# A graph build on TensorE: ranges read into registers once a tile, two blocks a table word, and a running counter

## The chip, the cores and the metric

One core of one Trainium2 chip. The metric is the device time of one execution in microseconds (us). The core's engines are TensorE (PE, with its weight loads PEld), VectorE (DVE), ScalarE (ACT), GpSimd (POOL) and SyncE (SP). Each has a sequencer that takes its instructions in order. Some of them never reach the engine behind it: register arithmetic, a load of registers from memory, branches, waits. In the trace these have the engine's name with a q (PEldq, DVEq).

## What is computed

Four graph layers over 1250 nodes of 512 features and 20,000 edges, each with a residual and a layer norm. Cut to what matters here:

```python
edge_index = stack([src, dst])                      # dst is sorted
x = layernorm(x + L0(x, edge_index, edge_weight))   # segment_sum(support[src] * weight, dst)
x = layernorm(x + L1(x, edge_index, edge_type_2))   # two relational layers: segment_sum over edges of each type
x = layernorm(x + L2(x, edge_index))                # normalised by degree
x = layernorm(x + L3(x, edge_index, edge_attr_8))   # attention over edges, 8 heads
```

The kernel does not gather rows of nodes. It first builds dense matrices of 1280 x 1280 (edge weights for L0 as a high and a low f16 part, edge counts of each of the two types for L1), and the layers are then matmuls with them. The change is in this build alone.

## The kernel before, in words

The 20,000 edges are 160 chunks (CH) of 125 edges, in the order of their destination. The destinations are 40 blocks of 32 nodes (TT = 40, CW = 32), four blocks to a tile (t4, 10 tiles). A block's rows of all matrices are a product: for each chunk that holds edges of the block, `own` (125 edges x 128: which of the 32 nodes, times four values) is PE's stationary operand, and a one-hot row over the 1250 other nodes is the moving one. DVE makes that row by comparing an iota with a key (line 878 for fixed visits, line 886 for further ones). One chunk is one visit: three matmuls of 512, 512 and 226 columns at line 1617, into three banks of PS.

A block has four fixed visits (FIXED = 4), and further ones in a loop whose length depends on the data. There are 44 further ones over 40 blocks: 36 blocks have one, four have two. The range of a block's chunks is worked out on the chip: a column of 40 words (first chunk, number of further visits, and an offset with which the running number of a further visit is the chunk plus the offset) is written to DRAM and read back into one row, `tab`. `tile_ranges` (line 436) loads four words into registers at each tile start, on DVE and on PE apart (line 439 is where the load and its checks stand in the trace). A range's shifts and masks are written where they are used.

The order of the work in one block on PE (`build`, line 1611): wait `evicted` (line 1626), first fixed visit, loop over the further visits (line 1628: wait `more_made`), then `fix` of the block before (line 1605: wait `copied`, three matmuls at line 1607 that take the copied high part off), then three fixed visits, and the signal `built`. ACT evicts each block twice: line 1320 copies 128 rows (signal `copied`; it waits for `built`), and line 1322, behind the fix, copies what is left in 32 rows (signal `evicted`). Blocks take turns on two sets of three banks, so block j waits for the eviction at line 1322 of block j-2; and the fix inside block j waits for the copy at line 1320 of block j-1. DVE (`make`, line 873) waits `built` of block j-2 for its eight fixed rows (HOTS), and `more_used` for its two further ones (MORE = 2). Semaphores are compared with registers (`wait_ge(more_made, v + 1)`). POOL's zero fills of a DRAM table (line 730) start on `built`; SP writes the evicted blocks out (lines 579 and 581) and starts the next weights' loads after the last.

The loops are loops of the chip, not unrolled: over the tiles (line 1644 on PE, lines 897 and 906 on DVE) and over the further visits (`Fori(lo + FIXED, hi)`). The build runs from 68.0 us, when PE's first matmul of it starts, to 243.6 us.

Of the kernel before, what the change touches and what calls it, by code (L numbers as in the profile page):

```python
# [8 lines left out]
I32 = mybir.dt.int32  # L9
ALU = mybir.AluOpType  # L10
# [10 lines left out]
EC = 125  # L21
CH = EDGES // EC
# [38 lines left out]
def gnn_resnorm(nc, a, out):  # L61
    ctx = ExitStack()
    with ctx:
# [11 lines left out]
        tab_d = dram("tab_d", (1, TT), I32)  # L75
# [45 lines left out]
        tab = in_w(TT)[0:1, :].bitcast(I32)  # L121
# [314 lines left out]
        def tile_ranges(eng, t4):  # L436

            ap = tab[:, bass.ds(t4 * 4, 4)]
            _, vals = nc.values_load_multi_w_load_instructions(ap, engines=(eng.engine,), min_val=0,
                                                                max_val=2 ** 31 - 1)  # L440
# [93 lines left out]
        def _(sp):  # L534
# [28 lines left out]
            sp.dma_start(tab_d[0, :].rearrange("(t k) -> t k", k=1), tabi[0:TT, 0:1]).then_inc(tab_out, 16)  # L563
            sp.wait_ge(tab_out, 17)
            sp.dma_start(tab, tab_d).then_inc(tab_in, 16)
# [207 lines left out]
        def _(dve):  # L773
# [9 lines left out]
            dve.sem_inc(more_made, CH)  # L783
# [60 lines left out]
            dve.wait_ge(ext_t, 2)  # L844
            step(V.tensor_tensor(bound[0:TT, 0:1], PS[0:TT, 3, 0:1], lohi[0:TT, 1:2], ALU.subtract))
            step(V.tensor_scalar(bound[0:TT, 0:1], bound[0:TT, 0:1], float(CH), None, ALU.add))
            V.tensor_copy(tabi[0:TT, 0:1], bound[0:TT, 0:1])
            V.tensor_copy(tabi[0:TT, 1:2], lohi[0:TT, 0:1])
            step(V.tensor_copy(tabi[0:TT, 2:3], visits[0:TT, :]))
            for k in range(2):  # L850
                step(V.tensor_scalar(tabi[0:TT, 0:1], tabi[0:TT, 0:1], 8, None, ALU.logical_shift_left))
                step(V.tensor_tensor(tabi[0:TT, 0:1], tabi[0:TT, 0:1], tabi[0:TT, k + 1:k + 2], ALU.bitwise_or))
# [19 lines left out]

            def make(rng, t4, j):

                lo, hi, off = rng
# [7 lines left out]
                with dve.Fori(lo + FIXED, hi) as c:  # L883
                    v = c + off
# [4 lines left out]
                for m in range(1, FIXED):  # L889
                    fixed(m)  # L890
# [1218 lines left out]
```

## Time and profile before

| | us |
|---|---|
| median of 3 runs | 1287.15 (1283.82 to 1288.16) |
| the profiled execution, its own time | 1289.35 |
| its span | 1287.6 |
| the build in it | 175.6, from 68.0 to 243.6 |
| PE busy, of the span | 1214.6 (94%) |
| DVE / ACT / POOL busy | 862.7 / 419.6 / 306.5 |
| granted TensorE clock, mean | 0.987 |

Some 1.8 us of the profiled execution lie around its span. A duration of a register instruction is its execution alone; the time from one to the next is longer, and the "issue" entries in the trace are idle time of an engine for which the trace shows no other releaser. A matmul's duration holds its passage through the array; the next one can start before it ends.

### The profile page before, as it was taken

The page shows a single profiled execution, that of the slowest core. Times are in us where ns is not written, and L with a number is a line of the kernel's source. Part 1 is how long each engine was busy: PE and PEld are TensorE (multiplying, and loading weights), DVE is VectorE, ACT ScalarE, POOL GpSimd, SP SyncE. Part 2 cuts the span into 40 slices and gives each one's busy share as a digit, 9 for nine tenths or more (in the row PEclk, how much of TensorE's full clock was granted, in tenths as well). Part 3 has the DMA queues.
Part 4 walks back from the last instruction along what each step waited for, and adds up shares of the span by engine and source line. Part 5 has one row for each costly group of instructions (what it writes and reads, how often), then busy time and mean ns, then how long its engine had stood idle before and what let it go on. Part 6 is the DMA issues. An engine that isn't in the chain of part 4 may idle for free.

```text
span 1287.6 us, 22149 instructions
## 1 busy us (share of the span) xinstructions
PE 1214.6 (94%) x8447; PEld 549.6 (43%) x8448; DVE 862.7 (67%) x1178; ACT 419.6 (33%) x564; POOL 306.5 (24%) x220
## 2 busy tenths in 40 slices
PE   6988888999898999999999999999999999999997
PEld 2333333333343334444444454453333555555553
DVE  7576665534434565562478873758999787978787
ACT  2445555522133122212301002154442343433432
POOL 2011010000010234354555555555461000000000
PEclk9989999999998999999999999999999999999999
DMA  8568886598698888734122212122323655556452
GB/s 307 217 220 264 283 290 186 191 395 314 217 371 294 292 287 271 257 76 131 14 38 34 50 20 49 2 24 32 43 32 100 221 206 197 169 182 207 154 181 103
DMA packets 64411, 222.77 MB, mean 173 GB/s; under 512 B 31224, under 2 KB 36088, under 8 KB 48358
## 3 DMA queue, kind: packets, MB, share of 16 engines
q1 hardware_dynamic: 34792, 156.40, 35.5%
q0 software_dynamic: 25184, 53.10, 16.5%
q10 hardware_dynamic: 4350, 12.07, 2.7%
q8 instruction: 63, 1.03, 0.3%
q14 instruction: 22, 0.18, 0.0%
HBM read 198.94 MB, written 59.94 MB: 201 GB/s over the span
## 4 chain that ended last, share of the span: by engine, by line
PE 72%; DVE 10%; issue 8%; DMA 7%; ACT 2%; DVEq 1%; SPq 1%; ACTq 1%
PE PS L1738 23%; PE PS L1687 10%; PE PS L1617 8%; PE PS L1983 5%; PE PS L1970 5%; PE PS L1553 4%; DVE R L1123 4%; PE PS L2016 3%; PE PS L1571 3%; PE PS L2003 2%; PE PS L1852 2%; PE PS L1607 2%; DMA W<-w_d 2%; DVE R L1158 1%; DMA w_d<-W 1%
## 5 line engine op out<-in xcount | busy, mean ns | idle before, releaser
L764 POOL DMA_INDIRECT bias_d<-R x160 | 268.8, 1680 | 333.1 <-DMA bias_d<-R 221.4
L1738 PE MATMUL PS<-R 128*128 128x512 f16 x1300 | 298.1, 381 | 0.0
L1738 PEld LDWEIGHTS PS<-R 128*128 128x128 f16 x1300 | 120.4, 98 | 180.7 <-issue 49.7
L1617 PE MATMUL PS<-R,XX 125*128 125x512 f16 (+2 forms) x612 | 130.9, 347 | 24.9 <-DVE R L878 16.1
L1518 ACT ACTIVATE R<-PS 128x1024 f32<-128x1024 f32 (+1 forms) x100 | 100.5, 1005 | 163.7 <-PE PS L1970 163.6
L1158 DVE SCALAR_TENSOR_TENSOR R<-R,W 128x1024 f32<-128x1024 f32 (+1 forms) x68 | 134.6, 1990 | 14.4 <-ACT R L1518 13.0
L1687 PE MATMUL PS<-W,XX 128*128 128x512 f16 x600 | 134.4, 383 | 4.8 <-DVE R L961 2.7
L878 DVE TENSOR_SCALAR R<-W,R 125x1250 f16<-125x1250 f16 x160 | 89.5, 606 | 46.9 <-PE PS L1617 43.3
L1123 DVE CUSTOM_DVE_ANT_0 R<-PS,R 128x1250 f16<-128x1250 f32 x80 | 116.8, 1459 | 5.5 <-PE PS L1906 2.9
L1983 PE MATMUL PS<-R 128*32 128x256 f32 (+1 forms) x1600 | 105.7, 382 | 5.0 <-DVE R L1158 4.2
L1970 PE MATMUL PS<-R 128*128 128x256 f16 (+3 forms) x800 | 106.0, 274 | 1.3 <-DVE R L1123 1.1
L730 POOL DMA_DIRECT2D bias_d<-bias_d x39 | 22.7, 589 | 324.7 <-PE PS L1617 153.5
L1617 PEld LDWEIGHTS PS<-R,XX 125*128 x612 | 57.5, 99 | 93.7 <-issue 57.0
L961 DVE SCALAR_TENSOR_TENSOR R<-PS,gate,R 128x512 f16<-128x512 f32 x50 | 37.4, 750 | 88.3 <-ACT R L1373 88.3
L1970 PEld LDWEIGHTS PS<-R 128*128 128x128 f16 (+1 forms) x800 | 71.6, 99 | 50.2 <-ACT R L1518 31.1
L1687 PEld LDWEIGHTS PS<-W,XX 128*128 128x128 f16 x600 | 57.8, 99 | 75.3 <-issue 7.5
L1158 DVE SCALAR_TENSOR_TENSOR R<-R 128x1024 f32<-128x1024 f32 (+1 forms) x32 | 63.6, 1993 | 9.3 <-ACT R L1518 5.5
L1322 ACT ACTIVATE R<-PS 32x1280 f32 x40 | 49.2, 1231 | 62.6 <-PE PS L1607 62.6
L1356 ACT ACTIVATE stat<-stat 128x1 f32<-128x1 f32 x30 | 8.8, 295 | 184.1 <-DVE stat L949 184.1
L1373 ACT ACTIVATE R<-PS,gate 128x512 f16<-128x512 f32 x50 | 34.4, 687 | 96.2 <-PE PS L1687 95.5
L1852 PE MATMUL PS<-XX,W 128*128 128x512 f16 (+1 forms) x288 | 61.3, 345 | 1.1 <-ACT R L1474 1.1
L1738 PE MATMUL PS<-W,XX 128*128 128x512 f16 x240 | 58.1, 387 | 3.0 <-issue 3.0
(220 smaller groups left out, 1357.0 us busy)
## 6 DMA issues: line engine op xcount, KB each, us to landing
bias_d<-bias_d POOLq DMA_DIRECT2D x39, 1280.0 KB, 10.7
R<-in_basis_s SPq DMA_DIRECT2D x32, 1024.0 KB, 6.8
W<-in_basis_s SPq DMA_DIRECT2D x28, 1024.0 KB, 6.6
W<-bias_d SPq DMA_DIRECT2D x27, 1024.0 KB, 4.9
R<-bias_d SPq DMA_DIRECT2D x13, 1024.0 KB, 4.8
R<-key_d SPq DMA_DIRECT2D x20, 500.0 KB, 3.7
R<-R SPq DMA_DIRECT2D x120, 80.0 KB, 6.3
W<-bias_d SPq DMA_DIRECT2D x7, 904.0 KB, 4.6
```

The lines of the kernel that those rows point to most:

```text
L764: pool.indirect_dma_start(bias_d, bass.IndirectOffsetOnAxis(ap=idx[:, c:c + 1], axis=0), attr[:, c, :], None, bounds_check=DUMP + GC * P - ...
L878: V.tensor_scalar(hot[0:EC, FIXED * (j % 2) + m, 0:NODES], iota16[0:EC, 0:NODES], base[0:EC, bass.ds(t4, 1), j], key[0:EC, bass.ds(lo + m, ...
L1123: V.tensor_tensor_reduce(out=junk[:, 0:NODES], in0=PS[:, b0:b0 + 3, :].rearrange("p a b -> p (a b)")[:, 0:NODES], in1=nmask[:, i, 0:NODES] ...
L1158: V.scalar_tensor_tensor(p, p, BIG, BR[t % NB].rearrange("p (r h) -> p h r", h=HEADS)[:, 4 * q:4 * q + 4, 0:w], ALU.min, ALU.mult).then_in ...
L1518: S.activation(ER[:, n % 4, :].rearrange("p (h r) -> p h r", h=4)[:, :, 0:w], PS[:, 2 * (n % 2):2 * (n % 2) + 2, :].rearrange("p a (e r) - ...
L1553: ins = T.matmul(PS[32 * c:32 * c + RELS * FT, MIXED(m), :], attbd[0:BJ, layer, :, :].rearrange("p r j -> p (r j)"), BASIS(m)[0:BJ, c, :], ...
L1617: ins = T.matmul(mm_out(3 * (j % 2) + b, p1 - p0), own[0:EC, bass.ds(c, 1), :, :].rearrange("p c m w -> p (c m w)"), hots(p0, p1), start=f ...
L1687: ins = T.matmul(mm_out(zi % 2, D), lhs, rhs, start=n == 0, stop=n == len(terms) - 1)
L1738: ins = T.matmul(mm_out(SUM_BANK(s, i), D), lhs, rhs, start=n == 0, stop=n == len(terms) - 1)
L1852: ins = T.matmul(mm_out(BANK_OF("q", g), hi - lo), W16[:, 1 + which, q, f, o_ * P:(o_ + 1) * P], XT16[:, p, f, lo:hi], start=n == 0 and f ...
L1970: ins = T.matmul(PS[:, 2 * (n % 2) + i // 2, (i % 2) * RB:(i % 2) * RB + w], key[:, h, j * P:(j + 1) * P], query[:, h, cols], start=k == 0 ...
L1983: ins = T.matmul(PS[32 * i:32 * i + 32, 4 + q, e * RB:e * RB + w], VA[:, j, 4 * q + i, 32 * e:32 * e + 32], ER[:, n % 4, i * RB:i * RB + w ...
```

## The change

1. A word of the table holds two blocks, 16 bits each (first chunk in the upper 8, further visits in the lower 8); the offset is gone, and with it the DVE steps that made it. The column is written to DRAM in 2-byte elements. DVE and PE load two words a tile, not four.
2. All four ranges of a tile are shifted, masked and kept in registers at the tile start, on both engines.
3. The loop over further visits runs from 0 to their count. Its running number is a register `visited`, which each engine adds one to at the loop's foot; `more_used` and `more_made` start from other values to match.

```diff
-        def tile_ranges(eng, t4):
-            ap = tab[:, bass.ds(t4 * 4, 4)]
+        def tile_ranges(eng, t4, regs):
+            ap = tab[:, bass.ds(t4 * 2, 2)]
...
-            for p in vals:
-                first = within((p >> 8) & 255, 0, CH - FIXED - 1)
-                end = within(first + (p & 255) + FIXED, FIXED + 1, CH)
-                ranges.append((first, end, eng.snap(p >> 16)))
+            for j in range(4):
+                part = []
+                for bit in (8, 0):
+                    reg = regs[len(part) + 2 * j]
+                    eng.reg_alu(reg, vals[j // 2], bit + 16 * (j % 2), ALU.logical_shift_right)
+                    eng.reg_alu(reg, reg, 255, ALU.bitwise_and)
+                    part.append(reg)
+                ranges.append((eng.snap(part[0], min_val=0, max_val=CH - FIXED - 1),
+                               eng.snap(part[1], min_val=1, max_val=CH)))
...
-            step(V.tensor_tensor(bound[0:TT, 0:1], PS[0:TT, 3, 0:1], lohi[0:TT, 1:2], ALU.subtract))
-            step(V.tensor_scalar(bound[0:TT, 0:1], bound[0:TT, 0:1], float(CH), None, ALU.add))
...
-                with pe.Fori(lo + FIXED, hi) as c:
-                    v = c + off
+                with pe.Fori(0, count) as n:
+                    v = pe.snap(visited, min_val=0, max_val=TT * CH)
                     pe.wait_ge(more_made, v + 1)
-                    visit(c, lambda p0, p1: flat(more[0:EC, bass.ds(v & (MORE - 1), 1), p0:p1]),
+                    visit(within(lo + FIXED + n, FIXED, CH - 1),
+                          lambda p0, p1: flat(more[0:EC, bass.ds(v & (MORE - 1), 1), p0:p1]),
                           False).then_inc(more_used, 1)
+                    pe.reg_add(visited, visited, 1)
```

(`make` on DVE changes in the same way.)

**PE at a tile's start** (tiles 1 to 9), from the table's load to the first visit's matmuls; an ISA row here is a check or several register operations packed into one instruction. Before:

```order
L439 TENSOR_LOAD W
L439 ISA x8
L1626 REGISTER_ALU
L1623 ISA [waits evicted]
L1617 REGISTER_ALU [waits hot_made]
L1617 REGISTER_ALU
L1617 ISA
L1617 MATMUL PS<-R,XX 128x512 x2
```

And now; the four rows behind the first L450 stand three times, for the ranges of the other three blocks:

```order
L440 TENSOR_LOAD W
L440 ISA x4
L447 REGISTER_ALU
L448 REGISTER_ALU
L447 REGISTER_ALU
L448 REGISTER_ALU
L450 ISA
L448 REGISTER_ALU
L447 REGISTER_ALU
L448 REGISTER_ALU
L450 ISA
...
L1633 ISA [waits evicted]
L1627 ISA [waits hot_made]
L1627 MATMUL PS<-R,XX 128x512 x2
```

Between the load and the first matmul stood 13 instructions, and now stand 23: half of the checks are gone, and 13 single register operations and four packed ones have come.

**PE at the loop over further visits** of any block. Before:

```order
L1628 ISA
L1628 UNCONDITIONAL_BRANCH
L1628 ISA
L1617 REGISTER_ALU [waits more_made]
L1617 ISA
L1617 REGISTER_ALU
L1617 MATMUL PS<-R,XX 128x512
...
L1628 REGISTER_ALU x2
L1628 ISA
L1628 COMPARE_AND_BRANCH
```

And now (a plain move of a register, which these rows don't show, stands ahead of the branch):

```order
L1638 UNCONDITIONAL_BRANCH
L1638 ISA
L1627 REGISTER_ALU [waits more_made]
L1627 ISA x2
L1627 MATMUL PS<-R,XX 128x512
...
L1644 ISA
L1638 COMPARE_AND_BRANCH
```

At the loop's foot three register instructions became one, and at its head one packed instruction became a move. A later block's start (blocks 1 to 3 of a tile) loses two of the four register instructions between its waits and its first matmul.

## Rows read from the trace of the kernel before

**Rows 1.** The page: the chain that ended last, by line.

```profile
PE PS L1738 23%; PE PS L1687 10%; PE PS L1617 8%; PE PS L1983 5%; PE PS L1970 5%; PE PS L1553 4%; DVE R L1123 4%; PE PS L2016 3%; PE PS L1571 3%; PE PS L2003 2%; PE PS L1852 2%; PE PS L1607 2%; DMA W<-w_d 2%; DVE R L1158 1%; DMA w_d<-W 1%
```

**Rows 2.** The build's stretch: busy time by engine (columns in its first row).

```profile
core 0: us, PE busy (x) PEld busy (x) DVE busy (x) ACT busy (x) POOL busy (x), PEclk, DMA share, GB/s
...
68.00:243.60 175.60, 152.25 (x730) 65.98 (x731) 116.15 (x210) 96.26 (x78) 15.35 (x24) 0.97 0.74 234
```

**Rows 3.** Line 1617, the build's matmuls: a sequencer instruction (ns), PE's idle time (us, count).

```profile
L1617 PEldq ALU_OP  x168: 32/36/47, 67.7 to 240.5; - x168
...
  issue: 65.3, 122
```

**Rows 4.** Timeline: blocks 2 and 3 of tile 4, start of tile 5 (start us, duration us).

```profile
149.72 1.23 ACT L1322 ACTIVATE R<-PS 32x1280 f32 x1 [1.19 <-PE PS L1607]
151.22 1.24 ACT L1320 ACTIVATE R<-PS 128x1280 f16<-128x1280 f32 x1 [0.26 <-PE PS L1617]
...
151.41 1.37 PE L1617 MATMUL PS<-R,XX 125*128 125x512 f16 x6 [0.23 <-issue]
...
152.83 0.70 PE L1607 MATMUL PS<-R,W 128*128 128x512 f16 x3
...
156.24 1.42 PE L1617 MATMUL PS<-R,XX 125*128 125x512 f16 x6 [1.13 <-DVE R L878]
```

**Rows 5.** Line 439 on PE's sequencer at the start of tile 5 (min/median/max ns).

```profile
L439 PEldq FUSED_REGOPS  x4: 146/152/168, 154.6 to 155.5; - x4
L439 PEldq SEQ_ASSERT  x4: 18/18/18, 154.8 to 155.7; - x4
L439 PEldq TENSOR_LOAD <-W x1: 434/434/434, 154.0 to 154.0; - x1
```

**Rows 6.** Line 1628, head and foot of the loop over visits, on PE's sequencer.

```profile
L1628 PEldq FUSED_REGOPS  x128: 41/78/157, 68.0 to 241.1; - x128
...
L1628 PEldq COMPARE_BRANCH  x44: 67/67/214, 69.3 to 241.2; - x44
```

**Rows 7.** Timeline of PE: a further visit behind the first.

```profile
109.27 0.69 PE L1617 MATMUL PS<-R,XX 125*128 x3 [0.69 <-issue]
```

**Rows 8.** Timeline of PE: tile starts (idle before in brackets), and one fix (L1607).

```profile
85.63 1.39 PE L1617 MATMUL PS<-R,XX 125*128 125x512 f16 x6 [0.83 <-issue]
...
174.73 1.42 PE L1617 MATMUL PS<-R,XX 125*128 125x512 f16 x6 [1.54 <-DVE R L878]
...
191.97 1.49 PE L1617 MATMUL PS<-R,XX 125*128 125x512 f16 x6 [1.73 <-DVE R L878]
...
198.73 0.70 PE L1607 MATMUL PS<-R,W 128*128 128x512 f16 x3 [0.36 <-ACT R L1320]
...
211.44 1.42 PE L1617 MATMUL PS<-R,XX 125*128 125x512 f16 x6 [1.22 <-DVE R L878]
...
228.06 1.39 PE L1617 MATMUL PS<-R,XX 125*128 125x512 f16 x6 [1.10 <-DVE R L878]
```

**Rows 9.** Timeline of ACT: the eviction ahead of that fix.

```profile
197.43 1.24 ACT L1320 ACTIVATE R<-PS 128x1280 f16<-128x1280 f32 x1 [1.35 <-PE PS L1617]
```

**Rows 10.** Timeline of DVE: the first two blocks of tile 2.

```profile
98.19 0.61 DVE L878 TENSOR_SCALAR R<-W,R 125x1250 f16<-125x1250 f16 x1 [1.24 <-PE PS L1617]
...
102.07 0.61 DVE L878 TENSOR_SCALAR R<-W,R 125x1250 f16<-125x1250 f16 x1 [0.95 <-PE PS L1617]
```

**Rows 11.** Line 439 on DVE's sequencer, all tiles.

```profile
L439 DVEq FUSED_REGOPS  x40: 183/186/224, 65.4 to 222.7; - x40
```

**Rows 12.** Busy time and granted clock (PEclk) behind three of PE's idle times.

```profile
175.40:179.00 3.60, 3.25 (x18) 1.51 (x18) 1.09 (x3) 1.56 (x2) 0.16 (x1) 1.00 0.77 200
193.20:196.60 3.40, 3.35 (x11) 1.33 (x10) 0.27 (x1) 1.23 (x1) 0.00 (x0) 0.50 0.71 172
328.40:335.00 6.60, 4.80 (x29) 1.27 (x29) 2.51 (x4) 2.39 (x4) 0.00 (x0) 1.00 0.26 41
```

**Rows 13.** Timeline of PE: the idle time at 328.4 us.

```profile
330.26 1.04 PE L1553 MATMUL PS<-R,attbd 120*8 120x512 f32 x8 [1.80 <-DVE W L929]
```

More of the change, by code:

```diff
@@ L9 @@
 I32 = mybir.dt.int32
+I16 = mybir.dt.int16
 ALU = mybir.AluOpType
@@ L120, in gnn_resnorm @@
         iota16 = in_w(NN // 2).bitcast(F16)
-        tab = in_w(TT)[0:1, :].bitcast(I32)
+        tab = in_w(TT // 2)[0:1, :].bitcast(I32)
         fix16 = in_w(P // 2).bitcast(F16)
@@ L843, in _ @@
             step(V.tensor_tensor(valA[0:EC, :, 2], wgt[0:EC, :], valA[0:EC, :, 3], ALU.subtract))
-            dve.wait_ge(ext_t, 2)
-            step(V.tensor_tensor(bound[0:TT, 0:1], PS[0:TT, 3, 0:1], lohi[0:TT, 1:2], ALU.subtract))
-            step(V.tensor_scalar(bound[0:TT, 0:1], bound[0:TT, 0:1], float(CH), None, ALU.add))
[L847 to L852, printed above, removed]
+            V.tensor_copy(tabi[0:TT, 0:1], lohi[0:TT, 0:1])
+            step(V.tensor_copy(tabi[0:TT, 1:2], visits[0:TT, :]))
+            step(V.tensor_scalar(tabi[0:TT, 0:1], tabi[0:TT, 0:1], 8, None, ALU.logical_shift_left))
+            step(V.tensor_tensor(tabi[0:TT, 0:1], tabi[0:TT, 0:1], tabi[0:TT, 1:2], ALU.bitwise_or))
             V.tensor_copy(inside[0:TT, 0:1], visits[0:TT, :]).then_inc(tab_out, 1)
@@ L871, in _ @@
             dve.wait_ge(tab_in, 16)
+            visited = dve.alloc_register("visited")
+            range_regs = [dve.alloc_register(f"range_{i}") for i in range(8)]
+            dve.reg_mov(visited, 0)
             def make(rng, t4, j):
-                lo, hi, off = rng
+                lo, count = rng
                 def fixed(m):
@@ L882, in make @@
                 fixed(0)
-                with dve.Fori(lo + FIXED, hi) as c:
-                    v = c + off
+                with dve.Fori(0, count) as n:
+                    v = dve.snap(visited, min_val=0, max_val=TT * CH)
                     dve.wait_ge(more_used, v + 1)
                     V.tensor_scalar(flat(more[0:EC, bass.ds(v & (MORE - 1), 1), 0:NODES]), iota16[0:EC, 0:NODES],
-                                    base[0:EC, bass.ds(t4, 1), j], key[0:EC, bass.ds(c, 1)], ALU.add,
+                                    base[0:EC, bass.ds(t4, 1), j],
+                                    key[0:EC, bass.ds(within(lo + FIXED + n, FIXED, CH - 1), 1)], ALU.add,
                                     ALU.is_equal).then_inc(more_made, 1)
+                    dve.reg_add(visited, visited, 1)
                 for m in range(1, FIXED):
@@ L892, in windows @@
             def windows(t4):
-                rngs = tile_ranges(dve, t4)
+                rngs = tile_ranges(dve, t4, range_regs)
                 for j in range(4):
@@ L1598, in _ @@
             pe.wait_ge(wl_made, M0)
-            pe.sem_inc(more_used, CH + MORE)
+            pe.sem_inc(more_used, MORE)
             pe.sem_inc(built, 2)
@@ L1609, in fix @@
                 ins.then_inc(fixed_up, 1)
+            visited = pe.alloc_register("visited")
+            range_regs = [pe.alloc_register(f"range_{i}") for i in range(8)]
+            pe.reg_mov(visited, 0)
             def build(rng, j, t4, first):
-                lo, hi, off = rng
+                lo, count = rng
                 def visit(c, hots, first):
```

12 lines of the change are left out of this document (5 added, 7 removed).

## The prediction, made before the changed kernel had run

> **What bounds the kernel now.** First the page's chain of waits by line: the build's matmuls (L1617) hold 8% and its fixes (L1607) 2% [rows 1]; the rest is layers that the change does not touch. Then the build as one stretch: 175.6 us, PE busy 152.25 of them, DVE 116.15 and ACT 96.26 [rows 2]. So PE sets the pace and 23.4 us of it are pauses (its idle time by releaser in one line: 65.3 us in 122 entries are "issue", which count what lies under a matmul's passage too, so they are no sum to save [rows 3]). Then the timeline, for where the pauses are. There are two kinds.
>
> At a tile's start PE stands 0.83 us (first of nine), 1.54, 1.73, 1.22, 1.10 (last) [rows 8]; the nine make a mean of 1.28. The trace puts most down to DVE's line 878, but DVE works two blocks ahead (it waits for `built` of block j-2): it makes the first row of tile 2 at 98.19, after 1.24 us of waiting for PE, and the next block's at 102.07, waiting again [rows 10]. The semaphore of DVE had long been there. What ends last is PE's own sequencer: the load of the ranges at 154.04 takes 0.434, eight checks and five further instructions follow, and the first matmul stands at 156.24 [rows 4, 5]: 1.77 us behind the load's end.
>
> Inside a tile a block takes about 3.9 us. The eviction of 32 rows ends at 150.95, the block's first matmul starts at 151.41: 0.46 of register work. ACT's copy ends at 152.46, the fix starts at 152.83 [rows 4]; where the fix had nothing else to wait for it came 0.06 behind the copy (198.67 to 198.73) [rows 8, 9]. So a ring of PE and ACT with about 0.3 us of register slack in it.
>
> **The price of a register instruction.** The 13 between load and matmul executed for 4 x 0.152 (checks), 4 x 0.018 (asserts) [rows 5], 3 x 0.036 [rows 3] and two small packed ones at 0.05: 0.89 us of the 1.77. The rest over 13 is 0.065 each between one and the next. So: single ALU 0.10, check 0.217, assert 0.083, packed from 0.106 (0.041 the shortest) to 0.233 (0.168 the dearest) [rows 5, 6]. The Trainium skill ("Perfetto Trace Analysis", Sequencer-only Instruction) says that the profiler shows the execution alone and that a hidden tail hangs on every sequencer operation; by execution alone the tile's start would lengthen by half as much as below, and the trace agrees with the page, half of the 1.77 being unseen.
>
> **Part by part.**
>
> 1. Table. The DVE steps for the offset lie in the preparation ahead of the build, with DVE waiting behind them, and the table lands long before 64 us: nothing, either way. If that cover were gone it would be some eight small DVE steps, under 1 us.
>
> 2. Ranges at a tile's start, PE. Now 2 checks (0.434), 2 asserts (0.166), 13 ALU (1.30), the last two packed (0.233) = 2.13, and four packed ones whose contents I can't see: 0.42 to 0.93 for the four; I take 0.73, 0.18 each, nearer the checks since they too pack a bound. 2.86 against 1.77: **+1.09 us a tile start** (bounds +0.78 to +1.29; below that only if single ALUs in a row overlapped, which the 0.065 says they do not). The load itself, two words instead of four, is one instruction before and after: no change taken. Nothing hides it, as PE waits for nothing else. Nine times: +9.8.
>
> 3. The same on DVE: its checks are dearer (0.186 each of 40 [rows 11]), four go a tile, the shifts come: about +0.9 us. DVE waits 1.24 and 0.95 us on PE in each block [rows 10], so it is hidden, but for tile 0, where PE waits for the first row: +0.3 net.
>
> 4. Counter, PE. Foot of the loop: two ALU fewer, -0.19. Head: the first packed one (0.078 median) becomes a move, the second (up to 0.157, it holds the offset's shift) gets lighter, a single one turns packed: -0.08 (0.04 to 0.12) [rows 6]. A visit's matmuls now stand 0.69 after the block's first ones [rows 7].
>
> 5. Start of blocks 1 to 3: two register instructions fewer between wait and matmul, -0.19.
>
> Could all of 4 and 5 be had, it were 0.27 in block 0 and 0.46 in blocks 1 to 3. But once the fix is 0.06 behind ACT's copy, ACT sets it: a one-visit block gives at most 0.37 - 0.06 = 0.3. I take 0.27, 0.17 (block 1, where the copy starts later), 0.30, 0.30: 1.04 a tile. So a tile is +1.09 - 1.04 = +0.05; nine: +0.5. The four blocks with two visits have more room (fix long behind the copy): 0.4 more each, -1.6. With tile 0's +0.3 the registers come to **-0.8 us**: a wash, gains inside tiles, losses at their starts.
>
> **What the longer pauses do to the clock.** This decides the sign. PE's granted clock stood at 0.50 for the stretch from 193.20, behind the pause of 1.73 before 191.97, and at 1.00 behind those of 1.54 (stretch from 175.40) and of 1.80 (before 330.26) [rows 8, 12, 13]. So near 1.7 us it can go either way. What it costs: tiles of two-visit blocks took 19.47 us (191.97 to 211.44) with the fall and 18.49 (156.24 to 174.73) without [rows 4, 8]; their closing pauses were 1.22 and 1.54, so a fall is worth 0.98 + 0.32 = 1.3 us. The new pauses are 1.28 + 1.09 = 2.37 in the mean (1.9 to 2.8): all longer than the one that fell. One of two around 1.75 fell; 2.37 lies further out than both, and tile 0's or a short pause behind it may save some. I take **4 of 9**, less the one there is: 3 x 1.3 = +3.9.
>
> Sum: -0.8 + 3.9 = +3.1. The profiled execution was 1289.35, its span 1287.6, and 2.2 above the median of 1287.15; the difference goes on the median: **1290.2 us**. Behind the build all waits for the last block's store, so a shift of its end passes on one to one; loads that have more time ahead could give some back, taken at nothing.
>
> **Rivals.**
>
> A. The clock falls at nearly every tile start (8 of 9), and packed instructions cost the upper value (nine times +0.2 = +1.8). 7 x 1.3 = 9.1, + 1.8 - 0.8 = +10.1: 1297.2. For it: every new pause is above 1.73, and a half-clock block makes its own ring longer. Against: 1.80 stayed at full clock. It is slower than before by more than can be told from about four additional falls on.
>
> B. No further falls, registers as worked out: 1286.4. The rise in pauses is 1.1 us and PE is over 80% busy around them; 1.54 and 1.80 did nothing.
> The Trainium skill ("TensorE: Matmul & The Clock Gate", What's actually happening) has the clock fall only after a window of idleness; pauses under 3 us, as here, would by it do nothing, so it speaks for B. The fall behind 1.73 us [rows 12] speaks against it.
>
> C. Faster: single ALUs in a row and the packed ones at their cheapest (nine times -0.31 = -2.8), registers -0.8, and the fall at 191.97 gone by a shift in phase (-1.3): -4.9: 1282.3. Nothing but luck in phase speaks for the last, the first needs packed ones as light as the lightest.
>
> D. DVE's longer chain reaches PE: only if it has less lead than 1.24 + 0.95 us somewhere; then nine times 0.9 = 8.1 less the registers' 0.8: +7.3, 1294.5. The waits of rows 10 speak against it.
>
> E. The change doesn't do what it says, for instance a range that makes an additional or a missing visit: the sum of visits comes from the same numbers, so it could only show as other matmul counts; I give it nothing.
>
> **How the numbers follow.** Forecast 0.38, A 0.26, B 0.20, C 0.12, D 0.04. About 3.9 us (0.3%) is what a measurement can tell from no change. Faster: C and a little of B with light packed ones, 0.18. Slower: A and D, and the part of the forecast with five or more falls, 0.37. Same: 0.45. The range runs from near C to A: 1283 to 1297; the likeliest case's own is 1287 to 1293.
>
> **What would show it.** PE's pauses at tile starts about 2.4 us (1.1 longer than before), the first matmul 2.9 us behind the load's end. In a block with one visit, the fix 0.06 to 0.1 behind ACT's copy; block period 3.6 to 3.7. The granted clock at 0.50 in about four places just behind tile starts; the build 173.5 to 183 us long, about 178.7. The DVE still waits for PE in each block. Wrong it would be if pauses stay under 2 us (the price of a register instruction), if the block's period stays at 3.9 (the ring), if the clock falls nowhere or everywhere, or if the time moves outside the build.

## The result, and the profile after

| | before | after |
|---|---|---|
| median, 20 runs each | 1287.39 | 1294.81 |
| ratio | 1 | 1.0049 (1.0036 to 1.0062), +6.3 us (the medians differ by 7.4) |
| the profiled execution's span | 1287.6 | 1293.6 |
| the build in it | 175.6, from 68.0 | 180.3, from 68.95 |
| mean granted TensorE clock, all runs | 0.9870 (17 runs) | 0.9821 (20 runs) |
| falls of the clock between tile 1 and the build's end | 1 | 6 |

The kernel became slower. The forecast was 1290.2, +3.1 and within what can't be told from no change; rival A said 1297.2. The time, 1294.8, is inside the range of 1283 to 1297, 4.6 above the forecast and 2.4 below rival A. The 17 runs of before with a clock are those of the first chip job below; all kernels of one job share them.

The page's chain by line, and the build as one stretch [rows 1, 2] (columns as there):

```profile
PE PS L1750 23%; PE PS L1699 10%; PE PS L1627 7%; PE PS L1995 5%; PE PS L1982 5%; PE PS L1559 4%; DVE R L1129 4%; PE PS L2028 3%; PE PS L1577 3%; PE PS L2015 2%; PE PS L1864 2%; PE PS L1613 2%; DMA W<-w_d 2%; DVE R L1164 1%; DMA w_d<-W 1%
```

```profile
68.95:249.24 180.29, 154.58 (x730) 68.76 (x731) 115.06 (x210) 96.22 (x78) 13.75 (x24) 0.93 0.71 228
```

The shares have hardly moved, and DVE and ACT are as busy as they were. The build is 4.7 us longer, and its granted clock fell from 0.97 to 0.93. What lies behind the build took 1044.4 us, against 1044.0: a shift passes on one to one, as said.

Line 1627 is what line 1617 was [rows 3]. PE has 44 single operations there in place of 168, yet more idle time under "issue":

```profile
L1627 PEldq ALU_OP  x44: 32/36/36, 69.4 to 245.9; - x44
...
  issue: 72.9, 115
```

Blocks 2 and 3 of tile 6 [rows 4] in the timeline (start us, duration us):

```profile
184.97 3.14 PE L1627 MATMUL PS<-R,XX 125*128 125x512 f16 x15
...
186.76 1.24 ACT L1326 ACTIVATE R<-PS 128x1280 f16<-128x1280 f32 x1 [0.25 <-PE PS L1627]
...
188.06 0.70 PE L1613 MATMUL PS<-R,W 128*128 128x512 f16 x3
```

ACT's copy ends at 188.00, the fix starts at 188.06: the 0.37 of before is now 0.06, what it was before only where nothing else held the fix. And from 184.97 to the next fix PE runs 15 matmuls over the block's border without a pause, where 0.2 stood. Inside a tile the counter and the prepared ranges did all that was forecast.

The start of tile 1, line 440 on PE's sequencer [rows 5], and then all tiles on both engines [rows 11]:

```profile
L440 PEldq TENSOR_LOAD <-W x1: 556/556/556, 83.5 to 83.5; - x1
```

```profile
L440 PEldq TENSOR_LOAD <-W x10: 538/898/1554, 64.3 to 231.5; - x10
L440 DVEq TENSOR_LOAD <-W x10: 544/547/1456, 64.4 to 227.3; - x10
```

From the load's end (83.49 + 0.556 = 84.05) to the first matmul (86.73) it is 2.68 us; 1.77 before. That was forecast as 2.86. But look at the load: two words take 0.547 us on DVE in the median, and on PE four of the nine at tile starts take 1.2 to 1.6. Before, with four words:

```profile
L439 PEldq TENSOR_LOAD <-W x10: 362/584/1032, 65.0 to 225.9; - x10
...
L439 DVEq TENSOR_LOAD <-W x10: 352/362/615, 64.8 to 221.5; - x10
```

I had put the load down as unchanged.

The loop over visits [rows 6]: each packed instruction of 0.078 or 0.157 is now 0.047, and the move is 0.029.

```profile
L1638 PEldq FUSED_REGOPS  x44: 47/47/52, 69.1 to 245.8; - x44
...
L1638 PEldq MOVE  x40: 29/29/37, 69.0 to 245.7; - x40
```

PE's nine tile starts [rows 8] (idle before in brackets):

```profile
86.73 1.43 PE L1627 MATMUL PS<-R,XX 125*128 125x512 f16 x6 [1.84 <-issue]
...
103.53 1.90 PE L1627 MATMUL PS<-R,XX 125*128 125x512 f16 x6 [2.24 <-issue]
...
123.06 1.33 PE L1627 MATMUL PS<-R,XX 125*128 125x512 f16 x6 [3.16 <-issue]
...
142.22 2.26 PE L1627 MATMUL PS<-R,XX 125*128 125x512 f16 x6 [2.98 <-DVE R L882]
...
160.07 1.36 PE L1627 MATMUL PS<-R,XX 125*128 125x512 f16 x6 [2.17 <-DVE R L882]
...
179.47 1.33 PE L1627 MATMUL PS<-R,XX 125*128 125x512 f16 x6 [2.14 <-DVE R L882]
...
196.78 2.26 PE L1627 MATMUL PS<-R,XX 125*128 125x512 f16 x6 [2.82 <-DVE R L882]
...
216.61 2.15 PE L1627 MATMUL PS<-R,XX 125*128 125x512 f16 x6 [3.09 <-DVE R L882]
...
234.75 1.33 PE L1627 MATMUL PS<-R,XX 125*128 125x512 f16 x6 [2.17 <-DVE R L882]
```

Their mean is 2.51 us, 1.28 before. Again most are put down to DVE, which is no more the cause than it was: at tile 2 its own register chain is now the 1.80 us ("issue"), and it still waits 3.17 us for PE within the tile [rows 10].

```profile
98.79 0.61 DVE L882 TENSOR_SCALAR R<-W,R 125x1250 f16<-125x1250 f16 x1 [1.80 <-issue]
...
105.86 0.61 DVE L890 TENSOR_SCALAR R<-W,R 125x1250 f16 x1 [3.17 <-PE PS L1627]
```

The clock [rows 12]: stretches behind pauses of 2.98, 2.17 and 2.14 us (tiles 4, 5 and 6), with the granted clock after the counts:

```profile
142.22:145.10 2.88, 2.88 (x8) 1.18 (x9) 0.00 (x0) 0.00 (x0) 0.00 (x0) 0.50 0.85 222
162.20:165.60 3.40, 3.40 (x12) 1.40 (x11) 1.83 (x4) 1.23 (x1) 0.00 (x0) 0.51 0.57 124
179.50:182.90 3.40, 3.40 (x18) 1.54 (x18) 0.78 (x2) 1.23 (x1) 0.00 (x0) 1.00 0.80 209
```

Six of the nine pauses were followed by a fall (tiles 2, 3, 4, 5, 7, 8), three were not (1.84, 2.14, 2.17).

### The profile page after: what moved, and what is told of

Read it like the earlier page. It is cut to its first block, busy times and chain, and to the rows that moved or that the text cites. A ratio compares the mean times of both kernels' runs of the same rounds, so it can differ in the third digit from the quotient of the medians.

```text
span 1293.6 us, 22050 instructions
## 1 busy us (share of the span) xinstructions
PE 1216.7 (94%) x8447; PEld 552.4 (43%) x8448; DVE 860.1 (66%) x1173; ACT 419.2 (32%) x564; POOL 307.6 (24%) x220
## 3 DMA queue, kind: packets, MB, share of 16 engines
q8 instruction: 63, 1.03, 0.3%
## 4 chain that ended last, share of the span: by engine, by line
PE 71%; DVE 10%; issue 8%; DMA 6%; ACT 2%; DVEq 1%; ACTq 1%; SPq 0%
PE PS L1750 23%; PE PS L1699 10%; PE PS L1627 7%; PE PS L1995 5%; PE PS L1982 5%; PE PS L1559 4%; DVE R L1129 4%; PE PS L2028 3%; PE PS L1577 3%; PE PS L2015 2%; PE PS L1864 2%; PE PS L1613 2%; DMA W<-w_d 2%; DVE R L1164 1%; DMA w_d<-W 1%
## 5 line engine op out<-in xcount | busy, mean ns | idle before, releaser
L770 POOL DMA_INDIRECT bias_d<-R x160 | 271.6, 1697 | 336.9 <-DMA bias_d<-R 224.0
```

Of the source, the lines that this page charges most:

```text
L770: pool.indirect_dma_start(bias_d, bass.IndirectOffsetOnAxis(ap=idx[:, c:c + 1], axis=0), attr[:, c, :], None, bounds_check=DUMP + GC * P - ...
```

## The experiments

Four kernels ran in each of the first two jobs and three in the last, with the kernel before run beside them. Times are medians; ratios are to the kernel before of the same job, with 95% intervals. Pauses, loads and falls are those of one profiled execution of each kernel. All have the tile loop, the blocks and the data as they were; none leaves out any of the computation.

| kernel | median, us | ratio | mean clock of its runs | PE's nine pauses at tile starts, sum in its profile, us |
|---|---|---|---|---|
| before (three jobs) | 1288.8, 1288.3, 1287.6 | 1 | 0.9870, 0.9870, 0.9873 | 11.5 |
| changed kernel | 1294.8 | 1.0049 (1.0036 to 1.0062) | 0.9821 | 22.6 |
| counter only | 1282.2 | 0.9953 (0.9938 to 0.9968) | 0.9865 | 11.3 |
| ranges only | 1296.6 | 1.0061 (1.0038 to 1.0084) | 0.9822 | 26.0 |
| ranges spread | 1279.2 | 0.9922 (0.9903 to 0.994) | 0.9863 | 11.4 |
| spread, load ahead | 1277.2 | 0.9903 (0.9884 to 0.9923) | 0.9880 | 0.4 |
| no checks | 1287.0 | 0.9991 (0.997 to 1.0012) | 0.9844 | 18.4 |
| no checks, rows of four | 1281.7 | 0.9947 (0.9926 to 0.9969) | 0.9860 | 13.8 |
| fillers | 1294.8 | 1.0055 (1.0038 to 1.0072) | 0.9849 | 27.0, fillers included |
| counter, no checks | 1276.6 | 0.9908 (0.988 to 0.9936) | 0.9880 | 2.9 |
| load ahead alone | 1281.7 | 0.9943 (0.9925 to 0.996) | 0.9884 | 7.3 |
| all, load in place | 1271.8 | 0.9876 (0.9847 to 0.9905) | 0.9885 | 3.0 |
| all, load ahead | 1272.9 | 0.9891 (0.9867 to 0.9914) | 0.9862 | 0.2 |

**The theory.** A tile's start is bound by PE's own sequencer; the ranges there lengthen it, the counter shortens the blocks, and the longer pauses let the clock fall. The rivals: the ring of evictions hides the counter's gain; DVE's name in the profile is right; the load is at fault; the falls come from somewhere else.

### One part alone: the counter

```diff
-                with pe.Fori(lo + FIXED, hi) as c:
-                    v = c + off
+                with pe.Fori(0, count) as n:
+                    v = pe.snap(visited, min_val=0, max_val=TT * CH)
...
+                    pe.reg_add(visited, visited, 1)
```

(and the same on DVE; the table and its load as before; `tile_ranges` hands on a block's count in place of its last chunk and its offset)

> Edit: the kernel before with the running counter alone; the table keeps its four words a tile (offset included, unread), and the load and its checks at a tile's start stay. My theory (register instructions priced at about 0.1 us apiece: the counter gains inside the tile, the ranges at the tile's start lose, the clock follows the pauses): tile starts 0.2 us shorter than before (9 x 0.2 = 1.8), 1.04 a tile inside (10.4), four two-visit blocks 1.6, the one fall of the clock gone half the time: -14 us against before, 1273, at most two falls of the clock in the build, pauses at tile starts 1.0 to 1.1 us. Rival 1 (the build is bound by the ring of evictions, the counter gives little): -3 us or less. Rival 2 (the tighter blocks themselves let the clock fall, not the pauses): falls at several tiles in spite of pauses near 1.1 us, and a time within 5 us of before.

6.6 us faster, less than half of what I expected; rival 1 (3 us or less) is refuted, since the build is 7.6 us shorter. PE's starts of tiles 2, 3, 8 and 9, and its loads:

```profile
102.22 2.26 PE L1622 MATMUL PS<-R,XX 125*128 125x512 f16 x6 [2.12 <-issue]
...
121.41 1.33 PE L1622 MATMUL PS<-R,XX 125*128 125x512 f16 x6 [1.83 <-DVE R L879]
...
205.29 1.33 PE L1622 MATMUL PS<-R,XX 125*128 125x512 f16 x6 [1.06 <-DVE R L879]
...
221.13 1.33 PE L1622 MATMUL PS<-R,XX 125*128 125x512 f16 x6 [1.05 <-DVE R L879]
```

```profile
L439 PEldq TENSOR_LOAD <-W x10: 329/392/1342, 64.8 to 219.0; - x10
```

The pauses are 1.03 to 1.26, close to the forecast, but for the first (0.72) and two behind loads of 1.34 and 1.11 us, and both of these were followed by a fall. They are the only two falls, so rival 2 (the tighter blocks themselves let the clock fall) is refuted as well. My expectation was also wrong in kind: I had credited the counter with the two register instructions that go at a block's start. They go because the *ranges* are ready. A tile of one-visit blocks took 14.8 us here (205.29 to 221.13, less the pause of 1.05), 15.5 before (211.44 to 228.06 less 1.10 [rows 8]) and 14.5 in the changed kernel: alone, the counter gives 0.7 of the 1.0 a tile. The next run shows that the rest is not simply the ranges' part.

### The other part alone: the ranges

```diff
-                first = within((p >> 8) & 255, 0, CH - FIXED - 1)
-                end = within(first + (p & 255) + FIXED, FIXED + 1, CH)
-                ranges.append((first, end, eng.snap(p >> 16)))
+                eng.reg_alu(first, p, 8, ALU.logical_shift_right)
+                eng.reg_alu(first, first, 255, ALU.bitwise_and)
+                eng.reg_alu(end, p, 255, ALU.bitwise_and)
+                eng.reg_add(end, end, first)
+                eng.reg_add(end, end, FIXED)
+                eng.reg_alu(off, p, 16, ALU.logical_shift_right)
+                ranges.append((eng.snap(first, ...), eng.snap(end, ...), eng.snap(off, ...)))
```

> Edit: the kernel before with its ranges alone moved into registers at the tile's start on both engines (first, end and offset of four blocks: 24 single register operations and four packed ones), the old loop and the four-word table kept. A large dose of the suspected cost. My theory: pauses at tile starts +2.6 us (24 x 0.097 + 4 x 0.13 less two that go), about 3.9 us; nine times = +23, falls of the clock at 8 or 9 tile starts: +10, shorter block starts and loop heads give 4 to 6 back: about +28 us, 1315. Rival 1 (register work at a tile's start is hidden behind DVE's wait, as the profile names DVE as releaser): within 5 us of before. Rival 2 (pauses cost, the clock does not): +18, 1305. DVE's chain grows too, by about 2 us a tile; it waits about 1.1 us per block on TensorE, so it could reach TensorE here, and the pauses would be longer than 3.9 us.

1296.6: slower, but by 8 us and not 28. The start of tile 4, its longest pause, then tile 6 (one-visit blocks): its start, a fix, and the start of tile 7:

```profile
145.89 2.27 PE L1628 MATMUL PS<-R,XX 125*128 125x512 f16 x6 [3.81 <-DVE R L887]
...
184.26 1.28 PE L1628 MATMUL PS<-R,XX 125*128 125x512 f16 x6 [2.72 <-DVE R L887]
...
189.16 0.70 PE L1616 MATMUL PS<-R,W 128*128 128x512 f16 x3
...
201.40 0.97 PE L1628 MATMUL PS<-R,XX 125*128 125x512 f16 x4 [2.71 <-DVE R L887]
```

The pauses grew to 2.88 in the mean, by 1.6 and not 2.6 us: the 24 operations that I counted in the source had become nine single instructions and four packed ones of 0.20 to 0.24. The price per instruction held (9 x 0.097 + 4 x 0.29 - 3 x 0.10 = 1.7); my count was of source lines. Rival 1 (hidden behind DVE) falls. The direction is the theory's: ranges at the tile's start alone make the kernel slower.

The other half of the miss is a gain. Tile 6 takes 14.43 us less its pause (184.26 to 201.40 less 2.71), with the old loop and its offset, against 15.5 before, 14.8 with the counter alone and 14.5 in the changed kernel. The fix already stands 0.05 behind ACT's copy (which ends at 189.11). So the parts don't add inside a one-visit tile: 1.1 us for the ranges alone, 0.7 for the counter alone, 1.0 for both. Where the fix waits for ACT's copy alone, fewer register instructions win nothing more: on top of the ranges the counter shows no gain there. The old loop with the ranges spread over the blocks, which would price the counter in the faster kernels, was not run.

### The changed kernel with PE's ranges spread over the blocks

```diff
                 for m in range(1, FIXED):
                     ins = fixed(m)
+                    if m == 1 and j < 3:
+                        rngs.append(one_range(pe, vals, j + 1, range_regs))
```

(`one_range` holds the same four shifts and masks and the two snaps; block 0's stays at the tile's start; DVE is not touched)

> Edit: the changed kernel, but TensorE's sequencer makes the range of block j+1 inside block j, between the matmuls behind the fix; only block 0's range stands at the tile's start, the two-word load and its checks too. DVE is as in the changed kernel. My theory: 9 of 13 single instructions and 3 of 4 packed ones leave the tile's start: 9 x 0.097 + 3 x 0.13 = 1.25 us less pause each, hidden where they now stand by matmuls already issued; pauses about 1.25 us (2.5 now), falls of the clock back to 0 to 2; against the changed kernel 9 x 1.25 = 11 and some 5 falls x 1.3 = 6: -17 us, so about 1277, 10 us faster than before. Rival 1 (the register work costs the same wherever it stands): no change from the changed kernel, 1294. Rival 2 (what lengthened the pauses is the load itself, 0.93 us in the mean against 0.585): pauses shrink by 1.25, but those with a load of 1.2 to 1.5 us stay near 2 us and keep the falls: about 1281.

1279.2, of 1277 forecast: 15.6 us faster than the changed kernel, by moving three ranges of PE a few matmuls back. That clears DVE, which is untouched: rival D is refuted by this run, and the releaser "DVE" in the profile was the label of a semaphore that had long come. Rival 1 is refuted too: at a tile's start the register work cost, and behind issued matmuls it cost nothing: the one-visit tiles 6, 8 and 9 take 14.45 to 14.53 us less their pauses, 14.49 in the changed kernel. Tile starts 2, 3 and 9:

```profile
103.83 1.33 PE L1634 MATMUL PS<-R,XX 125*128 125x512 f16 x6 [0.98 <-DVE R L887]
...
121.28 1.33 PE L1634 MATMUL PS<-R,XX 125*128 125x512 f16 x6 [2.09 <-issue]
...
220.71 1.33 PE L1634 MATMUL PS<-R,XX 125*128 125x512 f16 x6 [0.89 <-DVE R L887]
```

The two pauses of 2 us stand behind loads of 1.76 and 1.66; the clock fell behind the second of them alone. Rival 2 had 1281: the load has a part of its own.

### The load

Three runs on it. First the load of the next tile's words a block and a half ahead, on top of the spread ranges:

```diff
                 for m in range(1, FIXED):
                     ins = fixed(m)
+                    if m == 1 and j == 2:
+                        take(t4 + 1)        # load, checks, two moves
```

> Edit: as the kernel with spread ranges, and TensorE's load of the next tile's two words stands in block 2 behind the fix, with its checks; block 0's range of the next tile is made in block 3. Nothing of the ranges is left at a tile's start. My theory: the pause at a tile's start goes down to what is left at the loop's branch, under 0.3 us; a load of 0.55 us with its checks (1.2 us in all, 1.4 with two moves) behind 6 matmuls already issued (1.2 us) costs 0 to 0.3 us in block 2, and 0.5 to 1 more where the load takes 1.2 to 1.5; so -1.0 us a tile against the spread kernel: -9 us, and no fall of the clock: about 1268. Rival (the sequencer's load drains what is issued ahead, the pause only moves to block 2): the same time as the spread kernel, with a pause of 1.2 us or more in block 2.

The pauses are gone (0.4 us in all nine), and the time is 1277.2, only 2 us below the spread kernel, where 9 were expected. Half of the rival was right: the pause did move into block 2,

```profile
149.96 2.29 PE L1641 MATMUL PS<-R,XX 125*128 125x512 f16 x12 [0.54 <-DVE R L888]
152.51 0.70 PE L1619 MATMUL PS<-R,W 128*128 128x512 f16 x3 [0.27 <-ACT R L1332]
```

0.54 to 0.63 of idle time in each of tiles 1 to 9, again under DVE's name (no DVE instruction had moved). In the tile shown the fix and the three matmuls behind it keep PE busy from 148.18 to 149.42, 1.24 us; the sequencer's work from the fix on (the load's address, the load, the checks, the moves, the next visit's addresses) lets the next matmul start at 149.96, 1.78 us. Besides, ACT's copies now had to wait for stores, once for 3.78 us; PE's waits for ACT in the build add up to 8.9 us, 2.1 in the spread kernel. On this more at the end.

Then the same on the changed kernel, with all four ranges left at the tile's start:

> Edit: the changed kernel, but TensorE loads the next tile's two words (with their checks) in block 2 behind the fix; all four ranges still stand at the tile's start. It separates the load from the register work. My theory (two things lengthened the pauses: the register work, and a load that takes 0.55 us instead of 0.36 and at some tile starts 1.2 to 1.8, where SP's issue of the store at 2 to 3 us lies beside it): all of TensorE's loads take 0.53 to 0.60, the pauses fall from 2.5 to about 1.0 with none above 1.3, block 2 gets 0.7 us longer (1.2 us of load and checks behind 1.2 us of issued matmuls at the kernel with the load ahead), falls of the clock 0 to 3 instead of six: 9 x 1.5 = 13.5 less 7, and 4 x 1.2 = 5 for the clock: -11, 1283. Rival (the long loads come from the chip's memory traffic at large, wherever the load stands): loads of over 1 us appear in block 2 too, 1286 or more.

```profile
L442 PEldq TENSOR_LOAD <-W x11: 533/538/1242, 63.4 to 227.4; - x11
```

```profile
145.93 2.29 PE L1642 MATMUL PS<-R,XX 125*128 125x512 f16 x12 [0.54 <-DVE R L889]
...
151.59 1.35 PE L1642 MATMUL PS<-R,XX 125*128 125x512 f16 x6 [0.81 <-DVE R L889]
```

1281.7 against 1294.8, for 1283 forecast. The first load apart (1.24), all of PE's loads take 0.53 to 0.61, as on DVE; the rival, that they are long wherever they stand, is refuted. The pauses at tile starts are 0.81 to 0.85 in seven of nine (0.49 and 0.93 in the others), and 0.54 to 0.63 in block 2. There is no fall behind any of them.

Last, the load's width. `no checks` takes the check of each loaded word out; `rows of four` is the same with each tile's two words written twice, and the load takes all four:

```diff
             _, vals = nc.values_load_multi_w_load_instructions(ap, engines=(eng.engine,), min_val=-2 ** 31,
-                                                                max_val=2 ** 31 - 1)
+                                                                max_val=2 ** 31 - 1,
+                                                                skip_runtime_bounds_check_because="any 32 bits will do")
```

```diff
-            ap = tab[:, bass.ds(t4 * 2, 2)]
+            ap = tab[:, bass.ds(t4 * 4, 4)]
```

> Edit: the changed kernel without the run-time check that each loaded word lies between the smallest and the largest 32-bit number (two checks and two asserts on each engine a tile). My theory: a tile's start gets shorter by 2 x 0.217 + 2 x 0.083 = 0.60 us, pauses about 1.9 us; 9 x 0.6 = 5.4, one to three falls of the clock fewer at 1 to 1.3 us each: -5.4 to -9, so 1286 to 1290 against 1294.8. Rival (the long loads of 1.2 to 1.5 us set pauses and falls, not the instructions): pauses shorter by 0.6 but as many falls as before: -5.4.

> Edit: as the kernel without checks, but each tile's two words stand twice in a row of four, and the load at a tile's start takes all four words, of which two are used. The order of instructions is the same. It measures the load alone: with four words it took 0.35 to 0.36 us on DVE, with two 0.545. Theory (the time depends on the width or the alignment of the read, four words in 16 bytes going in one piece): 0.35 on DVE, pauses 0.2 us shorter than without checks, 9 x 0.2 = 1.8 us faster than it. Rival 1 (the load got longer by its surroundings in the changed kernel): 0.545 again, and the same time. Open in both: whether TensorE's loads of 1.2 to 1.5 us go; my guess is that some stay, since kernels with four-word loads had one or two of 1.1 to 1.5.

The loads without checks, of two words and then of four:

```profile
L440 PEldq TENSOR_LOAD <-W x10: 542/1140/1764, 64.5 to 226.5; - x10
L440 DVEq TENSOR_LOAD <-W x10: 541/546/1501, 64.7 to 222.2; - x10
```

```profile
L440 DVEq TENSOR_LOAD <-W x10: 352/354/1071, 64.1 to 212.9; - x10
...
L440 PEldq TENSOR_LOAD <-W x10: 330/438/1192, 64.0 to 217.1; - x10
```

Without checks it is 7.8 us faster than the changed kernel (5.4 to 9 were expected), with four falls in the build's profile instead of six. The rival's 5.4 is too close for the times to tell apart (the interval is 2.7 us to either side); the mean clock of the runs, 0.9844 for 0.9821, speaks for fewer falls. With the *wider* load of the same words, another 5.3 us: 0.354 on DVE against 0.546, whatever the tile, the first apart. On PE the sum over tiles 1 to 9 is 5.2 us against 9.6. I had expected 1.8. The load's time goes with what is read, as in the theory, and rival 1 is refuted; width and alignment were not separated, though two words took 0.544 to 0.556 us at even and odd tiles alike, while the read's start moves by 8 bytes a tile. Part of the 5.3 us is that there were fewer long loads, and since four-word loads were long in other kernels too (the counter's), how much of that is the width and how much is chance stays open.

What makes a load on PE long was not settled. In the changed kernel SP is issuing the stores of an evicted block when it starts; the rows at tiles 3, 6 and 9 (two issues each):

```profile
118.13 4.57 SPq L587 DMA_DIRECT2D R<-R  x2
...
175.56 5.07 SPq L587 DMA_DIRECT2D R<-R  x2
...
230.81 1.23 SPq L587 DMA_DIRECT2D R<-R  x2
```

How long SP issues doesn't sort them. The loads of 1.55, 1.45 and 1.38 (tiles 3, 8 and 4) lie beside rows of 4.6, 4.7 and 4.8 us, but those of 0.54 to 0.57 at tiles 1, 2, 5 and 6 lie beside rows of 5.0, 5.4, 4.4 and 5.1, too. What does hold in the profiles of the kernels with the load in block 2 is that none of those loads was long, and they lie beside single issues of 0.5 to 0.65. The cause stays open.

### The clock: fillers

```diff
+                if filler:
+                    filler[0]()      # one matmul of 512 columns on static operands, into an unused bank
```

(behind each of the four ranges at a tile's start)

> Edit: the changed kernel with one matmul more after each of the four ranges on TensorE at a tile's start, on static operands into a bank of PS that the build does not use; its result is read by nobody. Four matmuls of 512 columns, 0.21 us of TensorE each, and 16 single register operations instead of 13. The pause keeps its length and gets longer by 0.3 + 4 x 0.1 = 0.7 us, but TensorE works for 0.85 us of it. Theory (falls of the clock come from what the pause leaves undone): no falls in the build after the first tile, -6 x 1.1 to 1.3 = -7, against +0.7 x 9 = +6: about the time of the changed kernel, 1293 to 1296, with six falls gone. Rival (the pauses' length alone costs, the falls come from elsewhere): falls stay, +6 us: 1301.

```profile
83.94 0.39 PE L1625 MATMUL PS<-XX 125*128 125x512 f16 x1 [0.30 <-issue]
84.48 1.38 PE L1625 MATMUL PS<-XX 125*128 125x512 f16 x3 [0.16 <-issue]
```

These are the fillers of tile 1. From one tile's last matmul to the next one's first it is now 0.5 us longer each, fillers included, 4.4 in all, and the time is the changed kernel's, 1294.8. (The pauses had been put at 6 us longer, so that the time came out right is in part luck.) The mean clock of the runs rose from 0.9821 to 0.9849, and the falls in the build's profile went from six to four: pauses of 2.22, 2.53, 2.54, 2.68 and 3.31 us went without one, those of 2.79, 3.47, 3.70 and 3.78 did not. That profile is of its slowest execution (1299.97, clock 0.981, as low as the changed kernel's profile, with one fall more behind the build), so the runs' clock is the better witness. "No falls" was too much and the time was right. The rival (the falls come from elsewhere and stay; 1301) is refuted by the clock of the runs and the time.

### What helps, put together

```text
 counter, no checks: the counter alone (above), and the loads without checks
 all, load in place: spread ranges + no checks + rows of four
 all, load ahead:    the same, with the load in block 2
```

> Edit: the kernel before with the running counter, and without the run-time checks of the four loaded words (four checks and four asserts of 0.217 and 0.083 on each engine a tile). My theory: 4 x 0.30 = 1.2 us go from each tile's start; the pause there was 1.0 to 1.1 with a short load, so it all but disappears (0 to 0.2), and with a long load it is 0.8: 9 x 1.1 = 10 less than the counter alone, and no fall of the clock behind them (2 there in its profile): 1282.2 - 10 - 1 = 1271. Rival (something else stands close behind the register chain at a tile's start, the fix or DVE's first row): pauses stay above 0.5 us, 1276 or more.

1276.6 is the rival's time (1276 or more), but not by its mechanism: the pauses shrank to 0.21 wherever the load was short, so nothing stands close behind the register chain. In the profile they gave 8.4 us against the counter alone, but the tiles took 1.4 more in spite of two falls fewer. Most of that is a new wait: ACT's copies stand 6.0 us for stores to land, 1.5 with the counter alone, and PE's fixes behind them wait for ACT 4.2 us in place of 1.0. What lies behind the build took 1046.9 us against 1042.1, with two falls more there; at 1.3 us each (an estimate from the build's falls) that is half of it, the rest is open.

> Edit: all that helped, but the load left at the tile's start: running counter, ranges of TensorE made one block ahead, rows of four words, no run-time checks of the loaded words. Against the spread kernel (1279.2): 9 x (0.60 + 0.2) = 7, 1 us earlier start of the build, pauses about 0.4 to 0.5 with one or two near 1.3 where the load is long: about 1271.

> Edit: as the kernel before in this call, and the load of the next tile's row of four words stands in block 2. A load of 0.35 and two moves, 0.55 us, lie under 1.2 us of issued matmuls, so block 2 is no longer than the other blocks (3.6), and no pause at tile starts: tiles of 14.5 us (15.2 with a two-visit block), the build some 153 us long against 175.6 before, -22 us: 1266. Rival (something else than the registers comes due: DVE's first row at a tile's start, or ACT): pauses of 0.3 us or more under DVE's or ACT's name, about 1270, no better than the kernel with the load at the tile's start.

1271.8 and 1272.9: 1.2% and 1.1% faster than the kernel before, the two fastest. For the first the forecast was 1271, right in the time, though the build did not start 1 us earlier as was part of it (70.0, 69.7 in the spread kernel). For the second it was 1266, with a build of 153 us; that took 157.5, and the rival came in: nothing gained over the load in place. All its loads are short, and PE has no pause at any tile's start,

```profile
L441 PEldq TENSOR_LOAD <-W x11: 329/340/711, 64.1 to 219.9; - x11
```

but now this happens in several tiles:

```profile
82.15 5.63 SPq L596 DMA_DIRECT2D R<-R  x2
...
89.88 1.24 ACT L1335 ACTIVATE R<-PS 128x1280 f16<-128x1280 f32 x1 [2.45 <-DMA R<-R]
...
91.17 0.70 PE L1622 MATMUL PS<-R,W 128*128 128x512 f16 x3 [2.14 <-ACT R L1335]
```

SP is issuing stores of evicted blocks for 5.6 us (two issues), ACT's copy (L1335) waits for a transfer out of its staging buffer, and PE's fix waits 2.14 us for ACT. The shorter PE's pauses, the more of this there is: PE's waits for ACT in the build are 0.8 us in the kernel before, 4.9 with all and the load in place, 6.6 with the load ahead. This wait is the likely next bound of the build; no run took it away. The mean clock of the load-ahead kernel's runs, 0.9862 against 0.9885 over six runs each, is lower too, and its profile (0.988, no fall in the build) doesn't show where.

## Why the prediction came out as it did

**The bound at a tile's start: right.** PE's sequencer, and not DVE that the trace names. Shown by the spread kernel (-15.6 us with DVE's instructions unchanged).

**The price of a register instruction: right.** 2.68 us from load to matmul for 2.86 forecast, +0.91 for +1.09. The single ones kept 0.097 from start to start; the packed ones were 0.067 in the median, not 0.12, which is the whole difference.

**"No change taken" for the load: wrong.** It was 0.93 us in the mean of nine tiles after 0.585: +0.35 each, +3.1. With it the pauses grew by 1.23 each, +11.1 in all, for +9.8 forecast.

**The gain in the blocks: right, a little small.** Tile 6 took 15.51 us before (174.73 to 191.97 less the pause of 1.73) and 14.49 now (179.47 to 196.78 less 2.82): 1.02, for 1.04 forecast. Over ten tiles, with the two-visit blocks, -12.9 after the falls are taken out, for -11.0; the forecast had left out what tile 0 gains inside, 0.84 (16.78 to 15.94). That ACT's copy caps a block's gain is in the 0.06 behind it. The ranges alone reach that cap (14.43), so the split into the loop's part and the block start's says little about what either change is worth.

**DVE's chain: right.** Hidden in all tiles but the first; the build starts 0.9 us later (+0.3 forecast), since both engines' first loads took 1.3 and 1.5 us in place of 0.7 and 0.6.

**The clock: the mechanism right, the term too small.** I took four falls, there were six in the profile. A fall's price was near the forecast's 1.3: tiles 6 and 8, both of one-visit blocks, took 14.49 without and 15.97 with one; tile 4 took 15.68: 1.2 to 1.5. Five more falls make +6.5, where the sum had +3.9. The clock over all 20 runs points the same way without counting falls: it is 0.0049 lower in the mean, and among the runs of the changed kernel 0.001 of clock goes with 1.13 us. That is 5.5 of the 6.3 us. It also says that the changed kernel's profile has somewhat more falls than a usual run: five more falls went with 0.006 of clock from profile to profile (0.987 to 0.981), so 0.0049 is about four more in a usual run, an estimate.

So the term that was most off is the sum's last: +6.5 in the profile, some 5 in a usual run, for +3.9. The pauses had been forecast at 2.37 and were 2.51, the longest at 3.16 for "1.9 to 2.8"; long loads carried four of them to 2.8 to 3.2 us, and all four of these were followed by a fall. I had two points at 1.73 and 1.80 and put the new pauses, all longer, at less than even odds. Over the profile of the changed kernel: +0.9 start, +11.1 pauses, -12.9 blocks, +6.5 clock, +0.4 behind, 6.0 in all, which is the difference of the spans. (That it closes is no evidence: the blocks' term is what is left of the build after pauses and falls, with each fall at 1.3.)

**Rival B** (no more falls) would have given 1286.4. It was refuted by six falls behind pauses of 2.17 to 3.16 us. **Rival A** had the falls of eight tiles; there were six. The Trainium skill ("TensorE: Matmul & The Clock Gate", What's actually happening) has the fall come after a window of idleness, by which rival B would have been right. This case's trace doesn't agree: the six falls stand behind pauses of 2.17 to 3.16 us with busy stretches on both sides. The length of a pause doesn't decide it alone either: in the kernel with spread ranges and the load ahead PE waited 3.46 us for ACT inside a block (before the fix at 124.65), and no fall followed.

**The range** held the time. The measured change, +6.3 with an interval from 4.6 to 8.0, is clear of the 3.9 that was to count as no change, so it fell under slower, which had 0.37 beside 0.45 for same.

## What to carry to other kernels

Register work cost only where the sequencer had no matmuls issued ahead: put it behind the last wait of a block, a few matmuls before its use. Count instructions from the compiled order, not from the source, and look at what each register load asserts: checks that no 32-bit value can fail stood for 0.6 us of sequencer time in every tile. Run the parts of a change alone: inside a one-visit tile the ranges won 1.1 us by themselves, as much as both together, and the counter 0.7 without longer pauses. When a change lengthens the pauses of TensorE, price the fall of the clock behind them, 1.2 to 1.5 us each here. Over the profiles, the fillers' apart, no tile start's pause up to 1.63 us was followed by one, 8 of the 15 between 1.7 and 2.3 were, and 12 of the 16 from 2.4 on. Where it fell, the fall cost more than the 0.91 us of register instructions that the change had put there. And the releaser named for a pause is the semaphore that came last, not what the engine was doing: look at the sequencer's own rows first.

## What had not been expected of the hardware

- Loading two words into registers from SBUF took 0.545 us, loading four 0.34 to 0.36, on DVE in the median and in every kernel of either kind. The first load of each kernel, 0.6 to 1.5 us, is apart from this.
- The load of two words on PE took up to 1.8 us at a tile's start and 0.53 to 0.61 a block and a half earlier. Why is open.
- Four matmuls of 0.21 us put into each pause raised the mean granted clock of the runs from 0.9821 to 0.9849; falls still followed four of the nine pauses in the profile.
